# Attention and two feed-forward stages on one core: softmax sums through the row-maximum ring, weights laid out beforehand, Wo prepared during attention

## The chip, the cores and the metric

The kernel runs on one core of one Trainium2 chip. The metric is the device time of one execution in microseconds (us). The core has five engines with queues of their own: TensorE (PE), VectorE (DVE), ScalarE (ACT), GpSimd (POOL) and SyncE (SP, which only issues DMAs here). They meet at semaphores.

## The reference

Input x is 2 x 1024 tokens of 1024 channels, 2048 rows in all, in float32. Three layers follow one another:

```python
x = x + 0.5 * ffn(layernorm(x))      # gate top-2 of 8, base 1024x1024, LoRA rank 16 per expert
x = x + attn(layernorm(x)) @ Wo      # 32 heads of 32, 8 kv heads, RoPE, causal softmax over 1024 keys
x = x + 0.5 * ffn(layernorm(x))      # the same weights again
```

with `ffn(h) = h @ base_w.T + base_b + 2 * sum_e w_e * (h @ A_e.T) @ B_e.T`, where `w` is the softmax over the two largest gate logits, and `attn` computes softmax(q k / sqrt(32)) v for groups of four query heads that share a key and value head.

## The kernel before

Float32 precision is kept by splitting each operand of the large products into a high part (float32r, rounded by ScalarE) and a low part (the rest, by VectorE or GpSimd); `split_products` issues three matmuls for each pair (L48 to L50). Four stages run one after the other: f1 and f2 are `ffn_stage`, between them stand `qkv_stage` and `attention_stage`.

**ffn_stage** goes over 16 tiles of 128 rows. For a tile t: layer norm on VectorE (L520 writes `h`), eight transposes on TensorE (`turn_h`, L360), split into `hT_hi` (ScalarE, L453) and `hT_lo` (VectorE, L524), then the product with the wide weights `wt` (1024 base, 128 LoRA, 8 gate columns = 1160) in three parts of columns, `base(t, ., 2)`, `base(t, ., 0)`, `base(t, ., 1)`, the routing on VectorE, `turn_low`, and `lora`. The weights of part 2 of tile t+1 are used right after `lora(t)`.
- In f1 (`prep`) the weights come as they are given. Ten pieces plus the LoRA up-projection are loaded into `raw`, transposed on TensorE into PSUM (`turn_raw`, L349), and split from there (L448, L499). Only then does `base(0, ., 2)` begin. Both parts are later stored to `copy`, a piece per tile. Tiles also split a piece of `Wq` each.
- In f2 (`attn`) the tile first gets its attention projection, `project`, 48 matmuls with `wo_hi` and `wo_lo`, added to x (L559). Wo is loaded and split at the start of f2, piece by piece (L463, L566), with the projections of tiles 0 and 1 following each piece. The split feed-forward weights are loaded from `copy` during the attention stage.

**attention_stage** takes 16 steps n, one for each pair of batch and key head; a step has 12 units u of up to 512 queries by 128 keys: units 0 to 3 are the first half of the queries, 4 to 11 the second; 0 to 3 and 8 to 11 lie on the diagonal and have 512, 384, 256, 128 queries (4 to 7 have 512). Each unit has four heads g.
- *Row items.* Exponentials need each query's maximum beforehand. For the step n+1, 48 row products (L1232) go into a ring of three PSUM banks (`SLOTS`) and VectorE takes their maxima (L1376); two transposes of the maxima (L1227) go through the same ring. These items are spread over the units of step n.
- *Units.* In the turn of unit u, TensorE issues the scores of unit u+2 (L1242; three banks), each g followed by its portion of row items, and then `products(u)`: four products with the values (L1257) and, for u not in 4 to 7, four with `ones` (L1264) for the softmax sums, each group of four side by side. ScalarE takes exponentials of the scores (L1313) into `probs`, four buffers, unit u in buffer u % 4.
- GpSimd masks the diagonal units (L1165). It adds the buffers of units 4 to 7 (three additions of 128 x 2048, L1187), and their sum is taken by one set of `ones` products at u = 10 (L1269).
- After units 3 and 11 ScalarE copies the context and the sums from PSUM (L1319, L1321). VectorE transposes the sums, takes reciprocals and transposes them back (L1385 to L1391), GpSimd multiplies (`divide`, L1171), ScalarE takes the high part, GpSimd the low part (`low`, L1175), SyncE stores.
The order of each engine's queue is written out by hand; the first step and the last ones stand outside a loop of three steps per pass.

Of the kernel before, what the change touches and what calls it, by code (L numbers as in the profile page):

```python
# [72 lines left out]
def ffn_stage(nc, name, x_src, x_dst, fw, base_b, consts, prep=None, attn=None):  # L73
# [4 lines left out]
    RAW = 4  # L78
    PIECE = KC * D // NT
    COPY = KC * WIDE // NT  # L80
    with ExitStack() as ctx:  # L81
# [5 lines left out]

        (wt_hi, wt_lo), (bt_hi, bt_lo) = fw["wt"], fw["bt"]
        if prep:
            raw = sb("raw", [P, RAW, D], F32)  # L90
            wq_raw = sb("wq_raw", [P, 2, PIECE], F32)
            wq_hi, wq_lo = prep["wq"]
        if attn:
            wo_hi = sb("wo_hi", [P, KC, D], F32R)
            wo_lo = sb("wo_lo", [P, KC, D], F32R)
            ctxT = sb("ctxT", [P, 2, 2, KC, P], F32R)
# [3 lines left out]
        wo_raw = [x_ring[:, 2, :], x_ring[:, 3, :], h[:]]  # L100
# [6 lines left out]
        eps = sb("eps", [P, 1], F32)  # L107
        top = sb("top", [P, 8], F32)
# [35 lines left out]
        turn_ps = [ps[:, 2 * i:2 * i + 2, :].rearrange("p a (c n) -> p (a c) n", n=P) for i in (1, 3)]  # L144


        items = ([("gate", 0), ("A", 0)] + [("base", o) for o in range(KC)] + [("B", 0)]) if prep else []
        EARLY = 2
        TURN_H = 4
        NEXT = 10  # L150

        def raw_count(i):

            return 16 * sum(1 for j in range(i + 1) if j % RAW == i % RAW and items[j][0] != "B")

        x_loaded = [sem(f"x_loaded{s}") for s in range(4)]
        if prep:
            raw_loaded = [sem(f"raw_loaded{s}") for s in range(RAW)]
            b_loaded = sem("b_loaded")
            raw_turned = sem("raw_turned")  # L160
# [4 lines left out]
        if attn:  # L165
            wo_loaded = [sem(f"wo_loaded{s}") for s in range(len(wo_raw))]
# [5 lines left out]
        CONSTS = 2 * 16  # L172
# [34 lines left out]
        def load_ctx(eng, t, par):  # L207
            for part, src in enumerate((attn["ctx_hi"], attn["ctx_lo"])):
                eng.dma_start(ctxT[:, par, part, :, :].bitcast(F32), src[bass.ds(t, 1), :, :, :].rearrange("t c p n -> p (t c) n")).then_inc(ctx_loaded[par], 16)  # L209

        def run_tiles(eng, step):

            with eng.Fori(0, NT // 4 - 1, 1) as i:
# [4 lines left out]

        def turned_view(n, kind):
            v = turn_ps[n % 2]  # L220
            return v[:, :, 0:E] if kind == "gate" else v

        def weight_view(kind, k, part):
            if kind == "base":
# [1244 lines left out]
```

## Time and profile before

| | |
|---|---|
| median of 3 runs | 1725.84 us (1725.3 to 1728.64) |
| the profiled execution | 1721.34 us, its span 1719.4 us |
| granted TensorE clock, mean | 0.965 |
| busy: PE, DVE, ACT, POOL | 1600.4, 937.7, 598.2, 600.4 us |
| stages, from to (us) | f1 0 to about 287, q/k/v to 594, attention to 1281, f2 to 1719 |

In the rows further down a time is measured from the start of the span. A row of the order of time gives the start, the duration, the engine, the line of the kernel, the operation, what it writes and reads with shapes, how many instructions are merged, and in brackets the idle time before it and who ended it.

### The profile page before, as it was taken

Reading aid. Unit: us, or ns where it says so; the run is one execution under the profiler, and the core shown is the slowest. Engines: PE = TensorE matmul, PEld = TensorE weight load, DVE = VectorE, ACT = ScalarE, POOL = GpSimd, SP = SyncE. Lnnn points to the kernel's source line nnn. Section 1 sums busy time; section 2 is a strip of 40 time slices with the busy share of each in tenths; the row PEclk is TensorE's granted clock in tenths of the full one; section 3 lists DMA queues with packets and bytes.
Section 4 is the critical chain, followed back from the end, with each engine's and each line's share of the span. In section 5 each row is a group of like instructions: output and inputs, shape, how many; then the busy total and the mean of one; then the engine's idle time right before and its main releaser. Section 6 shows DMA issues by size and latency. Waiting matters only on the chain. (4 is left out here: it accounts for less than half of the span.)

```text
span 1719.4 us, 30209 instructions
## 1 busy us (share of the span) xinstructions
PE 1600.4 (93%) x9464; PEld 1214.3 (71%) x9464; DVE 937.7 (55%) x2716; ACT 598.2 (35%) x1218; POOL 600.4 (35%) x387
## 2 busy tenths in 40 slices
PE   6999996999999799998998998999949999999999
PEld 5999995788888644444444444454427999999998
DVE  5454444546554477776776777777714333333333
ACT  3333231211120035655555555565543111111110
POOL 1222221433343215665665555555551101101000
PEclk9999997999999869999999999999988999999999
DMA  6333333342331643333333343333135133133130
GB/s 201 131 122 133 133 109 136 118 136 99 110 108 64 163 112 78 90 89 90 90 89 90 92 99 90 89 90 97 47 95 189 54 94 98 49 98 97 49 86 37
DMA packets 167755, 173.69 MB, mean 101 GB/s; under 512 B 50616, under 2 KB 119864, under 8 KB 167616
## 3 DMA queue, kind: packets, MB, share of 16 engines
q1 hardware_dynamic: 139456, 148.90, 30.2%
q10 hardware_dynamic: 28160, 23.07, 4.0%
q8 instruction: 70, 1.15, 0.3%
q14 instruction: 69, 0.57, 0.1%
HBM read 104.24 MB, written 67.17 MB: 100 GB/s over the span
## 5 line engine op out<-in xcount | busy, mean ns | idle before, releaser
L1313 ACT ACTIVATE at_probs<-at_ps 128x512 f32<-128x512 f32 (+3 forms) x768 | 327.0, 495 | 265.9 <-PE at_ps L1242 261.3
L1376 DVE CUSTOM_DVE_ANT_0 at_ps<-at_ps,at_score_mask 128x512 f32<-128x512 f32 (+3 forms) x512 | 292.8, 616 | 98.5 <-PE at_ps L1232 95.5
L1232 PE MATMUL at_ps<-at_ks,at_qs 96*128 96x512 f32 (+3 forms) x768 | 279.6, 389 | 34.2 <-DVE at_part_max L1376 13.1
L1242 PE MATMUL at_ps<-at_qs,at_ks 98*128 98x512 f32 (+3 forms) x768 | 278.5, 389 | 18.6 <-issue 9.6
L1242 PEld LDWEIGHTS at_ps<-at_qs,at_ks 98*128 98x128 f32 x768 | 141.7, 192 | 182.0 <-issue 98.3
L48 PE MATMUL f_ps<-f_wt_hi,f_hT_hi 128*128 128x400 f32 (+1 forms) x768 | 265.5, 346 | 4.8 <-DVE f_wt_lo L499 2.4
L49 PE MATMUL f_ps<-f_wt_lo,f_hT_hi 128*128 128x400 f32 (+1 forms) x768 | 261.4, 340 | 0.0
L50 PE MATMUL f_ps<-f_wt_hi,f_hT_lo 128*128 128x400 f32 (+1 forms) x768 | 261.0, 340 | 0.0
L1232 PEld LDWEIGHTS at_ps<-at_ks,at_qs 96*128 96x128 f32 x768 | 151.8, 198 | 82.5 <-DVE at_part_max L1376 29.4
L317 POOL TENSOR_TENSOR f_x_ring<-f_x_ring,f_half_bias 128x1024 f32<-128x1024 f32 x32 | 76.7, 2396 | 335.6 <-DVE f_h L520 335.1
L1257 PE MATMUL at_ps<-at_probs,at_vs 128*32 128x512 f32 (+3 forms) x1536 | 167.0, 507 | 0.0
L1376 DVE CUSTOM_DVE_ANT_0 at_ps<-at_ps,at_score_mask,at_part_max 128x128 f32<-128x128 f32 (+3 forms) x256 | 133.9, 557 | 59.5 <-PE at_ps L1232 46.1
L1165 POOL TENSOR_SCALAR_AFFINE_SELECT at_probs<-at_probs 128x512 f32<-128x512 f32 x128 | 81.5, 637 | 214.6 <-ACT at_probs L1313 213.7
L48 PEld LDWEIGHTS f_ps<-f_wt_hi,f_hT_hi 128*128 128x128 f32 x768 | 145.4, 189 | 6.6 <-DVE f_wt_lo L499 2.7
L1187 POOL TENSOR_TENSOR at_added<-at_added,at_probs 128x2048 f32<-128x2048 f32 x32 | 146.9, 4591 | 1.5
L49 PEld LDWEIGHTS f_ps<-f_wt_lo,f_hT_hi 128*128 128x128 f32 x768 | 145.7, 190 | 0.6
L50 PEld LDWEIGHTS f_ps<-f_wt_hi,f_hT_lo 128*128 128x128 f32 x768 | 145.1, 189 | 0.0
L48 PE MATMUL f_ps<-f_wo_hi,f_ctxT 128*128 128x512 f32 x256 | 103.3, 403 | 20.0 <-DMA f_ctxT<-scr_ctx_lo 18.8
L48 PE MATMUL qkv_ps<-qkv_hT_hi,wq_hi 128*128 128x512 f32 x256 | 101.5, 396 | 2.4 <-DVE qkv_hT_lo L889 2.4
L49 PE MATMUL f_ps<-f_wo_lo,f_ctxT 128*128 128x512 f32 x256 | 101.2, 395 | 0.0
L50 PE MATMUL f_ps<-f_wo_hi,f_ctxT 128*128 128x512 f32 x256 | 101.2, 395 | 0.0
L50 PE MATMUL qkv_ps<-qkv_hT_hi,wq_lo 128*128 128x512 f32 x256 | 100.3, 392 | 0.0
(123 smaller groups left out, 2402.6 us busy)
## 6 DMA issues: line engine op xcount, KB each, us to landing
at_qs<-scr_q_hi SPq DMA_DIRECT2D x30, 512.0 KB, 6.3
f_x_ring<-in_L_attn_resid SPq DMA_DIRECT2D x16, 512.0 KB, 3.9
x<-f_x_ring SPq DMA_DIRECT2D x16, 512.0 KB, 2.6
qkv_x_ring<-x SPq DMA_DIRECT2D x16, 512.0 KB, 3.3
scr_q_hi<-qkv_rope_hi ACTq DMA_DIRECT2D x32, 256.0 KB, 2.0
scr_q_lo<-qkv_rope_lo ACTq DMA_DIRECT2D x32, 256.0 KB, 2.3
scr_ctx_hi<-at_ctx_hi SPq DMA_DIRECT2D x32, 256.0 KB, 2.2
scr_ctx_lo<-at_ctx_lo SPq DMA_DIRECT2D x32, 256.0 KB, 2.5
```

What stands on the lines that cost most here:

```text
L48: pe.matmul(out, stat_hi, mov_hi, start=start, stop=False)
L49: pe.matmul(out, stat_hi, mov_lo, start=False, stop=False)
L50: return pe.matmul(out, stat_lo, mov_hi, start=False, stop=stop)
L317: pool.tensor_tensor(x_ring[:, u, :], x_ring[:, u, :], half_bias[:], ALU.add).then_inc(bias_added, 1)
L1165: pool.affine_select(out=tile, in_=tile, compare_op=ALU.is_ge, fill=0.0, base=0, pattern=[[0, G], [1, P]], channel_multiplier=-1).then_inc ...
L1187: pool.tensor_tensor(added[:], first, probs[:, u % PROBS, :, :], ALU.add).then_inc(added_done, 1)
L1232: pe.matmul(out[:, 0:keys], qs[0:KROWS, nm, i // QH, g, (i % QH) * P:(i % QH + 1) * P], ks[0:KROWS, nm, c * HALF:c * HALF + keys], start=T ...
L1242: pe.matmul(score_ps[(u * G + g) % BANKS][:, 0:z - a], ks[:, nm, j * P:(j + 1) * P], qs[:, nm, half, g, a - half * HALF:z - half * HALF], ...
L1257: last = pe.matmul(ctx_ps[g * DH:(g + 1) * DH, at], vs[:, nm, j, :], probs[:, u % PROBS, g, 0:z - a], start=j == 0, stop=u in LAST)
L1313: act.activation(probs[:, u % PROBS, g, 0:z - a], score_ps[(u * G + g) % BANKS][:, 0:z - a], ACT.Exp, scale=SCALE).then_inc(exp_done, 1)
L1376: dve.tensor_tensor_reduce(out=src, in0=src, in1=mask, scale=1.0, scalar=part_max[:, g, own] if c else -3.0e38, op0=ALU.add, op1=ALU.max, ...
```

## The change

Two changes are joined.

1. **Feed-forward weights and Wo.** The host lays out base_w, lora_A and gate_w as one matrix of 8 x 128 x 1160 (`ffn_w`), lora_B as 128 x 1024 and Wo by rows. `turn_raw` and everything of it goes. In f1 each of the eight chunks is loaded (`raw_view`, three places and the x ring's last two), split with a factor 0.5 by ScalarE and VectorE, and used at once: `pair_chunk` lets tiles 0 and 1 take each chunk as it comes, in six banks; 16 transposes of the identity go first (`WARM`). The raw layout is copied from DRAM to DRAM in place of the split parts. During attention Wo is loaded, a piece of 256 KB per step, and split by ScalarE (`high_wo`) and GpSimd (`low_wo`); the context of tile 0 is loaded in the last step. f2 starts with the projections of tiles 0 and 1, while the feed-forward weights are loaded and split (`high_landed`, `low_landed`).
2. **Sums.** The sums of a half are one item of the row ring, which has four banks now. `ones` products are no longer part of `products`; GpSimd adds units 0 and 1 (a copy and an addition) and units 4 to 8 (four additions), and one set `sums` before the products of units 3 and 11 takes `added` and the units left apart (2, 3; 9, 10, 11). VectorE transposes the bank itself; the copy L1321 goes. `probs` has five buffers with a table of users.

```diff
-    SLOTS = 3
+    SLOTS = 4
-    PROBS = 4
+    PROBS = 5
-    ADDED = range(4, 8)
-    SUMMED = 10
+        ADDED = {0: 2, 1: 2, 4: 3, 5: 3, 6: 4, 7: 5, 8: 6}
+        APART = ((2, 3), (9, 10, 11))
+        ADDS = 6
+        USERS = ((0, 5, 8), (1, 7), (2, 6, 9), (3, 10), (4, 11))
+        PROB = {u: s for s, users in enumerate(USERS) for u in users}
+        BEFORE = {u: users[i - 1] for users in USERS for i, u in enumerate(users)}
...
+        for u, half in LAST.items():
+            places[u].append(("sum", half))
...
             def exps(n, u, g):
                 if g == 0:
-                    act.wait_ge(unit_done, NU * n + (u + 1))
-                    if u - PROBS in ADDED:
-                        act.wait_ge(added_done, (len(ADDED) - 1) * n + max(u - PROBS - ADDED[0], 1))
+                    v = BEFORE[u]
+                    earlier = NU if v < u else 0
+                    act.wait_ge(unit_done, NU * n + (earlier + 1 + (LAST_OF[units[v][0]] if v in APART[units[v][0]] else v)))
+                    if v in ADDED:
+                        act.wait_ge(added_done, ADDS * n + (ADDED[v] + (ADDS if earlier else 0)))
...
             def add(n, u):
-                pool.wait_ge(exp_done, NU * G * n + (G * (u + 1) + BANKS))
-                if u == ADDED[1]:
-                    pool.wait_ge(unit_done, NU * n + (PROBS + SUMMED + 1 - NU))
-                    first = probs[:, ADDED[0] % PROBS, :, :]
+                here = probs[:, PROB[u], :, :]
+                if u in diagonal:
+                    pool.wait_ge(mask_done, len(diagonal) * n + (diagonal.index(u) + 1))
                 else:
-                    pool.wait_ge(added_done, (len(ADDED) - 1) * n + (u - ADDED[1]))
-                    first = added[:]
-                pool.tensor_tensor(added[:], first, probs[:, u % PROBS, :, :], ALU.add).then_inc(added_done, 1)
+                    pool.wait_ge(exp_done, NU * G * n + (G * (u + 1) + BANKS))
+                if u == 1:
+                    before = probs[:, PROB[0], :, :]
+                    wait_apart(pool, unit_done, NU * n + NU, passed)
+                    pool.tensor_copy(added[:, :, 0:P], before[:, :, 0:P]).then_inc(added_done, 1)
+                    pool.tensor_tensor(added[:, :, P:HALF], before[:, :, P:HALF], here[:, :, 0:HALF - P],
+                                       ALU.add).then_inc(added_done, 1)
+                    return
+                if u == QH + 1:
+                    pool.wait_ge(unit_done, NU * n + (NU + QH))
+                    before = probs[:, PROB[QH], :, :]
+                else:
+                    pool.wait_ge(added_done, ADDS * n + (ADDS + ADDED[u] - 1))
+                    before = added[:]
+                pool.tensor_tensor(added[:], before, here, ALU.add).then_inc(added_done, 1)
...
             def step(n, nm, _, more):   # GpSimd
                 for u in range(NU):
                     a = ahead(n, nm, u, more)
                     if a and a[2] in diagonal:
                         mask(a[0], a[2])
+                    if u == 0:
+                        add(n, 1)
                     if first_step_over(n) and u == 2:
                         divide(n - 1, 1)
-                    if u in (3, 4, 6):
-                        add(n, (5, 6, None, 7)[u - 3])
-                    if first_step_over(n) and u == 8:
+                    if u in (4, 5, 6, 8):
+                        add(n, {4: 5, 5: 6, 6: 7, 8: 8}[u])
+                    if first_step_over(n) and u == 5:
                         low(n - 1, 1)
                     if u == 9:
                         divide(n, 0)
+                    if u == 10:
+                        low_wo(n)
                     if u == 11:
                         low(n, 0)
...
+            def sums(n, half, q, slot):   # TensorE, before products(3) and products(11)
+                pe.wait_ge(slot_read, q + 1)
+                pe.wait_ge(added_done, ADDS * n + (ADDS + (2, ADDS)[half]))
+                pe.wait_ge(mask_done, len(diagonal) * n + (QH * (half + 1)))
+                for g in range(G):
+                    pe.matmul(slot_ps[slot][g * DH:(g + 1) * DH, :], ones[:], added[:, g, :], start=True, stop=False)
+                for u in APART[half]:
+                    a, z = queries(u)
+                    for g in range(G):
+                        last = pe.matmul(slot_ps[slot][g * DH:(g + 1) * DH, a - half * HALF:z - half * HALF], ones[:],
+                                         probs[:, PROB[u], g, 0:z - a], start=False, stop=u == LAST_OF[half])
+                last.then_inc(slot_filled, 1)
...
+            if prep:                      # TensorE, start of f1
+                ALL = (2, 0, 1)
+                for c in range(3):
+                    pair_chunk(0, c, ALL)
+                turn_h(1)
+                for c in range(3, 5):
+                    pair_chunk(0, c, ALL)
+                for c in range(4):
+                    pair_chunk(1, c, (2,))
...
+            if attn:                      # TensorE, start of f2
+                project(0, 0)
+                project(1, 1, first_ps)
```

SyncE, in f1, waits for `w_lo_done` of 1, 2, 3, 5 and 6 low parts before it loads chunks 4, 5, 6, 7 and the LoRA part; in each attention step it waits for `wo_lo_done` of the step before, ahead of the Wo piece.

## Rows read from the trace of the kernel before

**Rows 1.** window of the attention stage: us, busy of PE, PEld, DVE, ACT, POOL

```profile
594.00:1281.00 687.00, 631.85 (x4256) 324.87 (x4256) 486.60 (x1664) 378.64 (x897) 381.54 (x240) 0.96 0.36 89
```

**Rows 2.** TensorE in order of time, stage f1: start us, us, engine, line, out<-in

```profile
55.87 1.03 PE L360 MATMUL f_ps<-f_ident,f_h 128*128 128x128 f32 x8
...
71.02 1.04 PE L360 MATMUL f_ps<-f_ident,f_h 128*128 128x128 f32 x8
```

**Rows 3.** SyncE's queue, VectorE and TensorE in order of time, start of stage f2

```profile
1281.58 0.34 SPq L242 DMA_DIRECT2D f_ident<-in_identity  x1
...
1307.79 1.29 DVE L559 TENSOR_TENSOR f_x_ring<-f_ps,f_x_ring 128x512 f32<-128x512 f32 x2 [2.59 <-DMA f_x_ring<-x]
...
1311.31 0.81 DVE L520 TENSOR_SCALAR f_h<-f_x_ring,f_mv,f_rstd 128x1024 f32<-128x1024 f32 x1
...
1317.66 1.03 PE L360 MATMUL f_ps<-f_ident,f_h 128*128 128x128 f32 x8
...
1321.07 0.43 PE L48 MATMUL f_ps<-f_wt_hi,f_hT_hi 128*128 128x360 f32 x1 [2.37 <-DVE f_hT_lo L524]
...
1325.14 1.03 PE L360 MATMUL f_ps<-f_ident,f_h 128*128 128x128 f32 x8
...
1351.18 1.04 PE L360 MATMUL f_ps<-f_ident,f_h 128*128 128x128 f32 x8
```

**Rows 4.** DMA issues of the page: KB each, median us to landing

```profile
f_x_ring<-in_L_attn_resid SPq DMA_DIRECT2D x16, 512.0 KB, 3.9
```

**Rows 5.** groups of instructions by shape: busy us, mean ns of one, idle us before them

```profile
L1232 PE MATMUL at_ps<-at_ks,at_qs 96*128 96x256 f32 x128 | 41.3, 350 | 12.2 <-DVE at_part_max L1376 9.2 <-DVE at_neg_lo L1362 2.8
...
L566 DVE TENSOR_TENSOR f_wo_lo<-f_x_ring,f_wo_hi 128x1024 fp32r<-128x1024 f32 x6 | 7.4, 1226 | 19.2 <-ACT f_wo_hi L463 19.1
```

**Rows 6.** windows, the loads at the start of f1: last columns PEclk, DMA share, GB/s

```profile
5.00:10.00 5.00, 3.42 (x18) 2.96 (x19) 0.23 (x1) 2.03 (x3) 0.00 (x0) 1.00 0.93 333
```

**Rows 7.** TensorE in order of time, a steady attention step and the last one

```profile
868.34 0.41 PE L1242 MATMUL at_ps<-at_qs,at_ks 98*128 98x512 f32 x1
...
886.08 0.50 PE L1242 MATMUL at_ps<-at_qs,at_ks 98*128 98x512 f32 x1
...
1269.70 1.04 PE L1269 MATMUL at_ps<-at_added,at_ones 128*32 128x512 f32 x8
...
1270.56 0.40 PE L1257 MATMUL at_ps<-at_probs,at_vs 128*32 128x128 f32 x8
```

**Rows 8.** GpSimd in order of time, steady attention steps and the last one

```profile
846.57 4.68 POOL L1187 TENSOR_TENSOR at_added<-at_probs 128x2048 f32<-128x2048 f32 x1 [2.89 <-ACT at_probs L1313]
...
856.50 4.59 POOL L1187 TENSOR_TENSOR at_added<-at_added,at_probs 128x2048 f32<-128x2048 f32 x1
...
861.04 0.63 POOL L1165 TENSOR_SCALAR_AFFINE_SELECT at_probs<-at_probs 128x512 f32<-128x512 f32 x1
...
862.45 1.28 POOL L1175 TENSOR_TENSOR at_ctx_lo<-at_ctxn,at_ctx_hi 128x512 fp32r<-128x512 f32 x1
...
886.43 4.68 POOL L1187 TENSOR_TENSOR at_added<-at_probs 128x2048 f32<-128x2048 f32 x1 [2.73 <-ACT at_probs L1313]
...
930.12 4.69 POOL L1187 TENSOR_TENSOR at_added<-at_probs 128x2048 f32<-128x2048 f32 x1 [2.90 <-ACT at_probs L1313]
...
1252.34 4.68 POOL L1187 TENSOR_TENSOR at_added<-at_probs 128x2048 f32<-128x2048 f32 x1 [5.27 <-ACT at_probs L1313]
```

**Rows 9.** ScalarE in order of time, first exponentials of a step

```profile
867.59 2.07 ACT L1313 ACTIVATE at_probs<-at_ps 128x512 f32<-128x512 f32 x4 [2.29 <-PE at_ps L1242]
```

**Rows 10.** TensorE in order of time, two rows after longer idles

```profile
39.13 1.43 PE L360 MATMUL f_ps<-f_ident,f_h 128*128 128x128 f32 x8 [2.87 <-DVE f_bt_lo L503]
...
915.85 0.38 PE L1242 MATMUL at_ps<-at_qs,at_ks 98*128 98x256 f32 x1 [3.00 <-issue]
```

**Rows 11.** windows, granted clock in the column PEclk

```profile
917.00:918.00 1.00, 1.00 (x4) 0.91 (x4) 0.79 (x5) 0.57 (x3) 0.00 (x0) 0.50 0.72 197
...
1320.00:1325.00 5.00, 3.93 (x24) 3.93 (x25) 3.39 (x6) 1.58 (x2) 0.98 (x1) 1.00 0.00 0
```

More of the change, by code:

```diff
@@ L278, in _ @@
             if prep:
-                sp.wait_ge(w_lo_done, len(items))
-                for part in range(2):
-                    sp.dma_start(prep["copy"]["bt"][part], flat(fw["bt"][part]).bitcast(F32)).then_inc(copy_stored, 16)
+                sp.dma_start(prep["copy"]["bt"], prep["ffn_bt"]).then_inc(copy_stored, 16)
             def step(i, t, u, more):
@@ L377, in base, with pair_chunk @@
                     last.then_inc(gl_done, 1)
+            def pair_chunk(t, c, parts):
+                pe.wait_ge(hT_lo_done, t + 1)
+                pe.wait_ge(w_lo_done, c + 1)
+                for part in parts:
+                    cols = slice(PARTS[part].start, WIDE if part == 2 else PARTS[part].stop)
+                    last = split_products(pe, pair_ps[t][part], hT_hi[:, t, c, :], hT_lo[:, t, c, :],
+                                          wt_hi[:, c, cols], wt_lo[:, c, cols], c == 0, part == 2 and c == KC - 1)
+                    if part == 2 and c == KC - 1:
+                        last.then_inc(gl_done, 1)
             def turn_low(t, more):
@@ L1053, in portions @@
         def portions(u, items):
+            items = [(p, it) for p, it in items if it[0] != "sum"]
             n = len(items)
@@ L1131, in _ @@
             load_rows(0, 0, at_a)
-            for part in range(2):
-                sp.dma_start(flat(fw["bt"][part]).bitcast(F32), copy["bt"][part]).then_inc(fw_loaded, 16)
             def step(n, nm, _, more):
@@ L1137, in step @@
                 if more >= 2:
-                    sp.wait_ge(unit_done, NU * n + PROBS)
+                    sp.wait_ge(unit_done, NU * n + NU)
                     load(n + 2, (nm + 2) % RING)
-                for part in range(2):
-                    sp.dma_start(flat(fw["wt"][part])[:, bass.ds(n * PIECE, PIECE)].bitcast(F32),
-                                 copy["wt"][part][:, bass.ds(n * PIECE, PIECE)]).then_inc(fw_loaded, 16)
+                sp.wait_ge(wo_lo_done, n + 1)
+                sp.dma_start(wo_raw[:], wo_src[:, bass.ds(n * PIECE, PIECE)]).then_inc(wo_loaded, 16)
+                if not more:
+                    for half in range(2):
+                        sp.wait_ge(ctx_stored[half], 32 * NKV + 16)
+                    for part, name in enumerate(("ctx_hi", "ctx_lo")):
+                        sp.dma_start(first_ctx[:, part, :, :].bitcast(F32), scr[name][0].rearrange("c p n -> p c n")).then_inc(ctx_loaded, 16)
                 if more:
@@ L1209, in _ @@
             low(NG - 1, 1)
+            pool.wait_ge(wo_lo_done, NG + 1)
         @block.tensor
         def _(pe):
[L1213 removed]
+            for count, start in ((slot_read, SLOTS), (exp_done, BANKS), (unit_done, NU), (added_done, ADDS), (recipT_done, 1),
                                  (ctx_copied, 1), (recip_done, 1), (mult_done, 1), (rows_loaded[0], 16),
@@ L1295, in step @@
                         slot_items(g)
+                    if u in LAST:
+                        p = position(("sum", LAST[u]), more)
+                        sums(n, LAST[u], SEQ * n + (PRE + p), (PRE + SEQ * nm + p) % SLOTS)
                     products(n, nm, u)
```

508 lines of the change are left out of this document (280 added, 228 removed).

## The prediction, made before the changed kernel was run

> **What bounds the kernel now.** I read four views: the busy shares by stage, the waits, the order of time at both feed-forward starts, and one steady attention step on each engine. In the attention stage TensorE is busy for 632 of 687 us, VectorE for 487, GpSimd for 382 [rows 1]: TensorE sets the pace, with GpSimd at 56%. At the start of f1 it is another limit: TensorE transposes weights and waits for their splitting. The bulk of the two feed-forward stages and the q/k/v stage is TensorE back to back and isn't changed. So the change has three places: the start of stage f1, the attention step (16 times), and the start of stage f2.
>
> **Start of f1.** Removed: ten weight pieces through TensorE transposes and PSUM, loaded before tile 1's work could begin. The marker is the set of eight transposes of tile 3, now at 71.02; a steady tile takes 71.02 - 55.87 = 15.15 us [rows 2]. Before that marker TensorE must, after the change, do tiles 0 and 1 (30.3) and the first product part of tile 2 (about 3.9, the stretch from 1321.07 to the transposes ending the part, 1325.14 [rows 3]): 34.2 us. The earliest start: x issued at about 1.3 and landing 3.9 later [rows 4], a layer norm of 3.0 (the 4.3 from 1307.79 to the end of the row at 1311.31, less two additions of 0.65), then 3.4 from transposes to first product (1317.66 to 1321.07) [rows 3]: 11.6. If TensorE never waited, the marker would stand at 45.8. It will wait: VectorE makes nine low parts of about 1.39 us (1.226 for 1024 columns [rows 5], times 1160/1024), beside two layer norms and two splits of transposed tiles, and the raw ring has four places, so chunks 4 to 7 are loaded only as low parts finish. By that list chunk 3 is ready at 18.4, chunk 4 at 19.8, chunk 7 at 27, and TensorE is continuous from about 22. That adds 2.7. The loads are no limit: 333 GB/s was reached between 5 and 10 us [rows 6], 1.8 us for a chunk of 594 KB. Marker at 48.5, gain 22.5 us. Bounds: 45.8 gives 25; if every chunk waits 1 us more for its load, 17.
>
> **Start of f2.** Before, the stage begins with Wo loads at 1281.58 and reaches tile 1's transposes at 1325.14, 43.6 later [rows 3]; most of this is Wo landing and being split. Wo now is ready. TensorE starts at about +2.2 (the identity), and two projections follow. One costs 26.04 - 15.15 = 10.9 us (the f2 tile period, 1325.14 to 1351.18, less that of f1 [rows 2, 3]); the first gets 2 more for a low clock at the start (the granted clock is 0.50 to 1.00 after an idle, below). They end at +15.1 and, with tile 0's transposes, +27.0. Then VectorE is late: from +15.1 addition and norm (3.7), three low parts (4.2), the split of the transposed tile (1.2), three low parts (4.2), addition (1.3), the small low part (1.2), norm (3.0): +33.9, so tile 1's transposes at +34.1. Gain 9.4. Bounds: 6 if the loads of 6.8 MB run at 200 instead of 333 GB/s, 11 if VectorE's order costs less.
>
> **Attention: what goes.** A step loses two product sets with `ones`, one of 512 columns (0.86 us, 1269.70 to 1270.56 [rows 7]) and one of 384 (three quarters, 0.65): 1.5 us. The fourth bank removes part of the short waits for row maxima: the row items of 256 columns alone waited 12.2 us in 16 steps [rows 5], 0.76 a step, and I take 1.0 for all. If TensorE stayed the limit, a step would fall from 39.86 (846.57 to 886.43 [rows 8]) to about 37.3. ScalarE loses 2 copies of the sums and gains one Wo piece; it has pauses before its exponentials (2.29 [rows 9]) that cover this. SyncE's Wo load of 256 KB replaces 580 KB of weights; its new wait on `wo_lo_done` is for work of the step before. Behind it stand only row loads and stores, which come later.
>
> **Attention: what comes.** GpSimd gets a copy of 512 columns and an addition of 1536 for units 0 and 1, a fourth addition of 2048 for unit 8, and the low part of Wo. By rows that is 0.64 to 1.28 (a mask or a two-input row of 512 [rows 8]), 3.4, 4.55 and 1.28: about 10 more on 24, 34 of 39.9 us. That fits, so the total isn't the limit; I take 0.8 for the copy, which hides in either case. The Trainium skill, GPSIMD Engine Reference, section Engine selection, says that two-input elementwise work is about twice as slow on GpSimd as on VectorE and one-input work about line rate. The trace agrees as far as it goes: 0.63 for a mask of 512 columns, 1.28 for a two-input row of 512. By it the copy would be at the lower end, the sum stays as it is, and moving additions here is what it speaks against.
>
> What matters is the order. `exps` of unit 0 of the next step writes buffer 0, last used by unit 8 (`USERS`), so it now waits for the addition of unit 8, the last of the step. The first addition of the half, of units 4 and 5, waits for `unit_done` of unit 3, whose products now stand behind the first sum set. So a chain runs on GpSimd: additions 5 and 6 and mask 8 (846.57 to 856.50: 9.93), `low` of the step before (1.28, moved ahead from u = 8), addition 7 (856.50 to 861.04: 4.54), masks 9 and 10 (0.61 each), addition 8 (4.54): 21.5 us [rows 8]. TensorE's own way over that stretch, from the scores of unit 6 (886.08 [rows 7]) to ScalarE's first exponential of unit 0 (867.59 plus a step, 907.45 [rows 9]), is 21.4 before and about 19 after the sets of units 8 and 9 and the waits have gone. GpSimd arrives 2.6 us later. TensorE holds three score banks, so the fourth score of unit 0 stands until the first exponential is done. Queued behind it are all row items, and so VectorE.
>
> The rest of the loop is TensorE's: that fourth score (868.34) to the scores of unit 6 (886.08), 17.74 [rows 7]. Sets worth 3.67 us leave this part and sets worth 3.67 (1280 columns for half 1, 896 for half 0) enter it; four banks take away most of its waits, which I put at 0.8 of the 1.0 (the 256-column items lie here). The loop is 0.1 + 21.5 + 0.1 (to ScalarE) + 0.75 (exponential, to score four) + 17.74 - 0.8 + 0.1 = 39.5. So against 39.86 almost all the 1.5 us saved on TensorE is spent on waiting for GpSimd.
>
> **The clock.** An idle of 2.37 us before 1321.07 [rows 3] left the granted clock at 1.00 in that stretch [rows 11], 2.4 GHz; one of 3.00 before 915.85 [rows 10] was followed by 0.50, 1.2 GHz [rows 11], and after one of 2.87 before 39.13 [rows 10] eight transposes took 1.43 in place of 1.03 [rows 2], the like sign. The step around the second took 930.12 - 886.43 = 43.69 [rows 8], 3.83 over a plain one, so the fall cost 0.8 over its idle. The new idle, 2.0 to 3.1, lies between. I take a fall in about half of the steps at 1.0: a step of 40.0, +0.15. Fifteen intervals: +2.
>
> **The end of attention.** In the last step no rows stand between the sets. There 18.9 us lie between addition 5 and the last products (1252.34 [rows 8] to about 1271.2 [rows 7]); after, 21.5 + 0.6 (mask 11) + 2.15 + 0.25 = 24.5. VectorE transposing straight from the bank gives back about 2, and step 0 loses 0.65: +3.
>
> **Sum.** -22.5 - 9.4 + 2 + 3 = -27. The profiled execution took 1721.34 (span 1719.4) and would take 1694.5. The median of the runs, 1725.84, is 4.5 above it: 1699.
>
> **Rivals.** (1) TensorE stays the limit, the GpSimd chain being hidden: 15 x -2.55 = -38, less 32 at the starts, 3 back: 1659. For it: GpSimd is only 56% busy now. Against: addition times are steady at 4.54 to 4.69 [rows 8], and the chain counts them one by one. (2) GpSimd's chain with the clock never falling: 15 x -0.35 = -5 in place of +2: 1692. Falling every time at the full 1.0: 1707. (3) The starts give half, because loads and splits queue behind each other: 16 less gained, 1715. For it: ring places 4 to 7 depend on low parts. Against: 333 GB/s [rows 6]. (4) Slower: the low clock after each GpSimd stall outlasts the step's free part and hits products at half rate for 5 us, 2.5 lost each time; with the step at 42.0, 15 x 2.15 = +32 and 3, less 32: 1729. It decides above 2.1 us per step. Against: the marked fall cost 0.8.
>
> **Chances.** The GpSimd chain as forecast, clock between never and always falling (1692 to 1707): 70%. TensorE the limit, or nearly (1659 to 1685): 10%. Starts worth half: 14%. Slower: 3%. No gain measurable: 3%. The range 1680 to 1715 leaves out the far end of the first rival and the last two. Changes under 0.2% (3.5 us) aren't told from none: faster 94%, same 3%, slower 3%.
>
> **What would show it.** After: ScalarE idle before `at_probs` released by GpSimd `at_added`, about 2.5 us once a step; additions 5 to 8 nearly unbroken; a step period of 39.5 to 40.5; tile 3's transposes in f1 near 48.5; tile 1's in f2 some 34 after the stage's first load; granted clock under 1.00 behind some stalls. Wrong if the period is near 37 (the chain is shorter or starts earlier than unit 3's products), or if f1's marker is past 54.

## The result, and the profile after the change

The changed kernel takes 1749.35 us (median, 1743.87 to 1754.05), the kernel before 1727.24 on the same chips (1725.30 to 1728.88): ratio 1.0127, 95% interval 1.0094 to 1.0161 (further down, ratios have their interval in brackets). It is 1.3% slower, where 1.6% faster was predicted. The profiled execution has a span of 1748.9 us, 29.5 more than before.

The page of the changed kernel: span, busy us of each engine, TensorE's busy share and granted clock in 40 slices.

```profile
span 1748.9 us, 29557 instructions
...
PE 1602.6 (92%) x9136; PEld 1219.4 (70%) x9136; DVE 950.9 (54%) x2707; ACT 591.9 (34%) x1199; POOL 755.4 (43%) x451
...
PE   7999995999999799989889898999967999999999
...
PEclk9999996999999579898897888888888999999999
```

TensorE looks as busy as before, but the last row shows why this says little: through attention (slices 15 to 31) the granted clock is 0.7 to 0.9, and at half rate the same matmuls are busy for nearly twice as long (the eight of one sum set 1.94 us from 1138.32, 1.06 from 1109.02).

Where the time went, by markers: the first addition of units 4 and 5 starts at 625.31, 16.5 us earlier than before (641.86); from that addition to the same one of the last step it takes 655.85 us in place of 610.48, +45.4 (15 steps, a mean of 43.72 for 40.70); from there to f2's first load 34.8 in place of 29.2, +5.5; f2's start -6.6 (below); the rest of f2 +1.7. Together +29.5. So both starts gained, and attention lost twice as much as they brought.

One plain step of attention. GpSimd, ScalarE and TensorE in order of time (start us, us, engine, line, operation; in brackets the idle before and what ended it):

```profile
1111.07 4.69 POOL L1286 TENSOR_TENSOR at_added<-at_probs 128x2048 f32<-128x2048 f32 x1 [2.84 <-PE at_ps L1366]
1115.84 4.62 POOL L1286 TENSOR_TENSOR at_added<-at_added,at_probs 128x2048 f32<-128x2048 f32 x1
1120.42 1.28 POOL L1263 TENSOR_TENSOR at_ctx_lo<-at_ctxn,at_ctx_hi 128x512 fp32r<-128x512 f32 x1
1121.66 0.62 POOL L1253 TENSOR_SCALAR_AFFINE_SELECT at_probs<-at_probs 128x512 f32<-128x512 f32 x1
1122.27 4.59 POOL L1286 TENSOR_TENSOR at_added<-at_added,at_probs 128x2048 f32<-128x2048 f32 x1
1126.82 1.21 POOL L1253 TENSOR_SCALAR_AFFINE_SELECT at_probs<-at_probs 128x512 f32<-128x512 f32 x2
1128.01 4.52 POOL L1286 TENSOR_TENSOR at_added<-at_added,at_probs 128x2048 f32<-128x2048 f32 x1
...
1132.64 1.58 ACT L1430 ACTIVATE at_probs<-at_ps 128x512 f32<-128x512 f32 x3 [5.65 <-POOL at_added L1286]
...
1133.29 0.80 PE L1351 MATMUL at_ps<-at_qs,at_ks 98*128 98x512 f32 x1 [3.59 <-ACT at_probs L1430]
...
1154.18 4.69 POOL L1286 TENSOR_TENSOR at_added<-at_probs 128x2048 f32<-128x2048 f32 x1 [2.69 <-PE at_ps L1366]
```

This is the predicted chain: additions 5 to 8, a low part and masks without a pause from 1111.07 to 1132.5, then the exponential of the next step's unit 0, then the fourth score. Its length to ScalarE is 21.57 us (predicted 21.5 + 0.1). The other part of the loop, from ScalarE to the next step's addition of units 4 and 5, is 21.54 us where 17.9 was predicted. The windows show what it is made of (columns: stretch, its length, busy us of PE, PEld, DVE, ACT, POOL, granted clock, DMA share, GB/s):

```profile
1108.00:1112.00 4.00, 4.00 (x42) 2.30 (x41) 2.96 (x8) 2.67 (x6) 1.16 (x2) 1.00 1.08 236
1128.00:1132.00 4.00, 1.71 (x13) 0.86 (x5) 2.09 (x7) 0.00 (x0) 4.00 (x2) 1.00 0.00 0
1132.00:1136.00 4.00, 2.71 (x12) 1.25 (x13) 0.82 (x2) 2.60 (x5) 3.47 (x5) 0.52 0.00 0
1136.00:1140.00 4.00, 4.00 (x15) 1.98 (x17) 2.31 (x6) 1.85 (x4) 2.12 (x3) 0.50 0.01 4
1140.00:1144.00 4.00, 4.00 (x44) 2.20 (x37) 1.15 (x5) 1.04 (x4) 0.52 (x1) 0.70 0.44 131
1144.00:1148.00 4.00, 4.00 (x29) 1.99 (x30) 3.31 (x18) 1.73 (x8) 3.08 (x3) 1.00 0.15 39
```

After the idle of 3.59 us TensorE stands at 0.50 (1.2 GHz) and comes back to 1.00 only at about 1142, though it is busy without a break from 1133.29 on: some 9 us in which the products of unit 10, the next step's scores, row items and the sum set of half 1 go at half rate. This step is one of the worse ones. Of the 15, the clock stands at 0.50 for 10.2 us in five and for 6.8 in ten (688.4 to 695.2, for one). The waits of attention:

```profile
PE at_ps L1351 <- ACT at_probs L1430: 54.4, 20, 3.6
...
ACT at_probs L1430 <- POOL at_added L1286: 95.4, 28, 5.7
```

TensorE idles once in each of the 15 steps ahead of the same score, 2.94 us in the first and 3.54 to 3.59 in the others: 53 of the 54.4 us.

The two starts of the feed-forward stages, TensorE and SyncE in order of time:

```profile
36.97 0.33 PE L371 MATMUL f_ps<-f_ident,f_low_s 128*128 128x128 f32 x1 [2.34 <-DVE f_low_s L590]
...
52.95 1.06 PE L336 MATMUL f_ps<-f_ident,f_h 128*128 128x128 f32 x8 [1.08 <-DVE f_x_ring L630]
...
1315.93 0.35 SPq L238 DMA_DIRECT2D f_ident<-in_identity  x1
...
1317.83 0.79 PE L48 MATMUL f_ps<-wo_hi,first_ctx 128*128 128x512 f32 x1 [10.52 <-DMA f_ident<-in_identity]
...
1352.93 1.96 PE L336 MATMUL f_ps<-f_ident,f_h 128*128 128x128 f32 x8 [4.79 <-DVE f_h L560]
```

Tile 3's transposes of f1 stand at 52.95, 18.1 us earlier than before [rows 2] (22.5 predicted). Tile 1's of f2 come 37.0 us after the stage's first load, 43.56 before [rows 3], a gain of 6.6 (9.4 predicted): VectorE is the late one, as predicted, but its norm is 2.9 us later.

### The profile page after: what moved, and what is told of

Its sections match the earlier page's. It is cut to its first block and busy times, and to the rows that moved or that the text cites. A ratio compares the mean times of both kernels' runs of the same rounds, so it can differ in the third digit from the quotient of the medians.

```text
span 1748.9 us, 29557 instructions
## 1 busy us (share of the span) xinstructions
PE 1602.6 (92%) x9136; PEld 1219.4 (70%) x9136; DVE 950.9 (54%) x2707; ACT 591.9 (34%) x1199; POOL 755.4 (43%) x451
## 5 line engine op out<-in xcount | busy, mean ns | idle before, releaser
L1430 ACT ACTIVATE at_probs<-at_ps 128x512 f32<-128x512 f32 (+3 forms) x768 | 330.8, 494 | 241.8 <-PE at_ps L1351 140.8
L1351 PE MATMUL at_ps<-at_qs,at_ks 98*128 98x512 f32 (+3 forms) x768 | 297.4, 414 | 68.1 <-ACT at_probs L1430 58.5
L1351 PEld LDWEIGHTS at_ps<-at_qs,at_ks 98*128 98x128 f32 x768 | 154.0, 209 | 234.8 <-ACT at_probs L1430 181.0
L1286 POOL TENSOR_TENSOR at_added<-at_added,at_probs 128x2048 f32<-128x2048 f32 x48 | 220.2, 4588 | 1.5
L1341 PEld LDWEIGHTS at_ps<-at_ks,at_qs 96*128 96x128 f32 x768 | 162.1, 215 | 39.2 <-issue 12.4
L1366 PE MATMUL at_ps<-at_probs,at_vs 128*32 128x512 f32 (+3 forms) x1536 | 175.1, 531 | 9.0 <-POOL at_probs L1253 9.0
L1286 POOL TENSOR_TENSOR at_added<-at_probs 128x2048 f32<-128x2048 f32 x16 | 75.2, 4700 | 61.7 <-PE at_ps L1366 61.7
L49 PE MATMUL qkv_ps<-qkv_hT_lo,wq_hi 128*128 128x512 f32 x256 | 100.2, 392 | 0.0
L931 POOL TENSOR_TENSOR qkv_rot<-qkv_rot,qkv_sin 128x512 f32<-128x512 f32 x40 | 51.5, 1289 | 106.2 <-DVE qkv_rot L987 106.1
```

The lines of the kernel that those rows point to most:

```text
L49: pe.matmul(out, stat_hi, mov_lo, start=False, stop=False)
L931: pool.tensor_tensor(rot[:, g % 2, :], rot[:, g % 2, :], sin[:, cols], ALU.mult).then_inc(sin_done, 1)
L1286: pool.tensor_tensor(added[:], before, here, ALU.add).then_inc(added_done, 1)
L1341: pe.matmul(out[:, 0:keys], qs[0:KROWS, nm, i // QH, g, (i % QH) * P:(i % QH + 1) * P], ks[0:KROWS, nm, c * HALF:c * HALF + keys], start=T ...
L1351: pe.matmul(score_ps[(u * G + g) % BANKS][:, 0:z - a], ks[:, nm, j * P:(j + 1) * P], qs[:, nm, half, g, a - half * HALF:z - half * HALF], ...
L1366: last = pe.matmul(ctx_ps[g * DH:(g + 1) * DH, at], vs[:, nm, j, :], probs[:, PROB[u], g, 0:z - a], start=j == 0, stop=u in LAST)
```

## The experiments

Five theories ran against each other. **A**: the loss is GpSimd's chain, waited for once a step, and the clock that falls behind each wait. **B**: the additions are in the way wherever the wait stands. **C**: the four banks and the sum items slow the ring. **D**: the clock's fall costs nothing of its own. **E**: splitting Wo in attention costs the steps. Each ratio is to the kernel before, run beside it. A step is the time from one step's addition of units 4 and 5 to the next one's; "plain" leaves out the three ends of the loop's turns. The runs are from several chips, and the kernel before took 1725.4 to 1727.2 us beside all of them.

**Fill the idle time (D).** Ahead of the fourth score of unit 0, the one that waits:

```
if a and a[2] == 0 and g == G - 1:
    ...
    pe.wait_ge(slot_read, SEQ * n + (PRE + p) + 1)
    for _ in range(FILL):    # 14, or 7
        pe.matmul(slot_ps[...], ks[0:KROWS, nm, 0:P], qs[0:KROWS, nm, 1, 0, :], start=True, stop=True)
```

> The changed kernel with 14 spare products of 512 columns (about 3 us) into the row bank that is free at that point, ahead of the fourth score of unit 0 of the next step, the one that stands and waits. They change no result and lengthen TensorE's own work, but fill most of the idle time. Theory A: the GpSimd chain and the wait stay (step 39.5 to 40.2), but the clock stays at 1.00: 15 x 2.2 to 3 less, 1704 to 1716. Rival D (the clock's fall costs nothing of its own, since the step's length is that of the additions all the way round): within 5 us of 1749. If the spare products only add to TensorE's work: 1750 to 1795.

1701.09 us, ratio 0.9847 (0.9826 to 0.9869): 48 us below the changed kernel, by work that nobody needs. TensorE in order of time, and the windows over the same stretch:

```profile
1132.24 3.38 PE L1410 MATMUL at_ps<-at_qs,at_ks 96*128 96x512 f32 x14
1136.05 0.50 PE L1352 MATMUL at_ps<-at_qs,at_ks 98*128 98x512 f32 x1 [0.43 <-ACT at_probs L1437]
```

```profile
1132.00:1136.00 4.00, 3.62 (x16) 2.63 (x14) 1.41 (x4) 0.60 (x2) 4.00 (x3) 1.00 0.00 0
1136.00:1140.00 4.00, 3.95 (x29) 1.99 (x33) 2.49 (x7) 3.51 (x8) 3.33 (x4) 1.00 0.00 0
```

The score still waits for GpSimd, but the clock stays at 1.00, and the plain step is 39.3 us (additions at 1113.72 and 1153.05; 39.2 to 39.4 but for the first and the last), against 42.1 to 43.3 in the changed kernel; the prediction had put the loop at 39.5 with the clock kept. From the fourth score to the next step's first addition it is 17.0 us here (1136.05 to 1153.05) and 20.9 in the changed kernel (1133.29 to 1154.18), for the same products: the fall costs 3.9 us there and 3.2 in the mean step (43.72 for 40.51). Plain step by plain step it is 3.6 to 4.0 where the clock is low for 10.2 us and 2.8 to 3.2 where it is for 6.8. D is out.

> The changed kernel with 7 spare products (1.5 us) in place of 14 ahead of the score that waits, so that an idle of about 2.1 us is left in each step. Theory A: it is the idle's length that decides; 2.37 us left the clock alone at the start of f2, 2.94 with the low part moved did not: here it stays, 1698 to 1710. If it falls in some of the steps: 1710 to 1735. If any idle lowers it: 1735 to 1750.

1733.59 us, ratio 1.0044 (1.0026 to 1.0063; the ratio leaves out one of the ten runs, which took 5055.75 us, has no trace and stays unexplained; the median of the other nine is 1731.93). The idle left was 1.37 us in the first step and 1.96 to 2.03 in the others. The two steps of these windows had idles of 2.03 and 2.02 (ahead of 1115.11 and 1154.22):

```profile
1117.00:1121.00 4.00, 4.00 (x48) 2.05 (x47) 2.53 (x7) 1.83 (x6) 3.46 (x4) 1.00 0.01 4
1154.00:1158.00 4.00, 3.78 (x16) 2.40 (x17) 1.29 (x3) 3.32 (x8) 3.18 (x4) 0.60 0.00 0
```

The clock fell behind 11 of the 14 idles of about 2 us, for 3.4 or 6.8 us, and stayed behind three, the one ahead of 1115.11 among them. The expectation that 2 us are harmless was wrong; the middle one, a fall in some of the steps, gives the time.

**The wait itself.** First a sixth buffer, paid for with the 8 KB of f2's first context tile (f2 then loads that itself, and its first product comes 6.6 us after the stage's first load, not 1.9):

```
-    PROBS = 5
+    PROBS = 6
-    USERS = ((0, 5, 8), (1, 7), (2, 6, 9), (3, 10), (4, 11))
+    USERS = ((0, 6), (1, 7), (2, 8), (3, 9), (4, 10), (5, 11))
```

> The changed kernel with a sixth probability buffer (unit u in buffer u modulo 6), so that unit 0 of the next step follows unit 6 and no longer waits for the addition of unit 8; the 8 KB come from the context tile that attention loaded ahead for stage f2, which f2 now loads itself. Theory A (the changed kernel is slow because unit 0 of the next step waits for the additions 5 to 8 on GpSimd, and the gap of 3.6 us lowers the clock each time): gap and fall both vanish, TensorE is the limit again, the step goes from 42.6 to 37.3 to 38.5 us, 15 x 4.1 to 5.3 = 62 to 80 us less, 2 back at the start of f2: 1670 to 1690. Rival B (the additions on GpSimd are in the way wherever the wait stands, since the sum set of half 1 needs the addition of unit 8 too): the gap moves to that set, step 41 to 43, 1730 to 1752. Rival C (the five slower us of a step come from four row-maximum banks and the sum items in the ring, not from the buffers): within 5 us of 1749.

Then only another table for the five: `USERS = ((0, 7), (1, 5, 8), (2, 6, 9), (3, 10), (4, 11))`.

> The changed kernel with one line of its buffer table changed: users (0, 7) and (1, 5, 8) in place of (0, 5, 8) and (1, 7). Unit 0 of the next step now waits for the addition of unit 7, and unit 1 of the next step for that of unit 8. Theory A: unit 0 comes 4.5 us earlier, so without a stall; unit 1 follows it on TensorE by about 3.5 us, so at most about 1 us of stall is left, in two smaller parts, too short for a fall of the clock: step 38.5 to 40, 1749 - 15 x (2.6 to 4.1) = 1688 to 1710. Rivals B and C: within 5 us of 1749.

1730.93 us, 1.0026 (1.0006 to 1.0047), and 1728.21 us, 1.0011 (0.9993 to 1.0028): 18 and 21 us below the changed kernel, where A said 59 to 79 and 39 to 61. B looked the better theory. But with six buffers the wait for `at_added` was gone from ScalarE's list, yet TensorE idled 3.5 us a step as before (the waits of ScalarE and of TensorE):

```profile
ACT at_ctx_hi L1435 <- POOL at_ctxn L1253: 52.6, 15, 3.6
...
PE at_ps L1345 <- ACT at_probs L1424: 54.0, 20, 3.6
```

`high(n, 0)` stands in ScalarE's order ahead of the exponentials of the next unit 1, waits for GpSimd's `divide`, and `divide` stands behind the addition of unit 8. It is a second way from the same chain, hidden by the first. Hence two kernels that cut both: the one with six buffers, with `divide(n, 0)` ahead of the addition of unit 8, and the one with the other table, with `high(n, 0)` at u = 11:

> The six-buffer kernel with GpSimd's multiplication of half 0 by the reciprocals moved ahead of the addition of unit 8. In the six-buffer run unit 0 no longer waited, but ScalarE's high part of half 0 (queued ahead of the exponentials of unit 1 of the next step) waited 3.6 us a step for this multiplication, which stood behind the addition of unit 8. Theory A2 (two waits lead from GpSimd's additions into ScalarE's order; taking away one alone leaves the other, with the same gap and the same fall of the clock): now neither is left, TensorE is the limit: step 37.3 to 38.3, 1731 - 15 x 3.3 to 4.5, 1663 to 1682. Rival B2 (a third wait on the additions comes up, at the sum set of half 1): step 39 to 41.5, 1690 to 1730. Rival C (ring of four banks and sum items are slow by themselves): 1725 to 1735.

> The kernel with the changed buffer table (five buffers) and ScalarE's high part of half 0 moved behind the exponentials of unit 1 of the next step, so that nothing of the next step stands behind the multiplication. Left is the wait of unit 1 of the next step for the addition of unit 8, which was 1.0 us long for ScalarE. Theory A2: step 38 to 39.3, no fall of the clock, 1728 - 15 x 2 to 3.5 = 1675 to 1698. Rivals B2 and C: 1720 to 1735.

1697.42 us, 0.9845 (0.9823 to 0.9868), and 1709.66 us, 0.9914 (0.9886 to 0.9942). Rival B2 was right for the first: TensorE now waited 1.97 us a step at the sum set of half 1, for the mask of unit 11 behind the addition of unit 8. The second lies between A2 and its rivals, with waits of 1.3 us for unit 8's addition and of 2.0 to 2.6 us for a row load in some steps.

**The low part.** One line back to where it was before the change, behind the addition of unit 8 (`low(n - 1, 1)` at u = 8 in place of 5):

> The changed kernel with the low part of the step before (1.28 us on GpSimd) put back behind the addition of unit 8, where it was before the change: the chain of GpSimd is 1.28 us shorter, nothing else is altered. Theory A: 15 x 1.28 = 19 us less, 1730, and if the gap of then 2.3 us no longer lowers the clock, as one of 2.37 did not, 15 x 2.4 more, 1694. Rivals B and C: within 5 us of 1749.

> The same, with the low part of the step before also behind the addition of unit 8, so that this addition ends 1.28 us earlier and the 1.0 us wait of unit 1 goes. Theory A2: 0 to 15 us below the kernel without this move; the two at the same time if TensorE sets the step in both: 1668 to 1695.

1731.44 us, 1.0027 (1.0014 to 1.0041), 18 us less where 15 x 1.28 gives 19, with the clock falling behind idles of 2.77 to 2.95 just the same; as A said for that case. On the table with the moved high part: 1697.49 us, 0.9864 (0.9824 to 0.9905), 12 us less and just above the forecast.

**The third way.** Six buffers, high part at u = 11, low part behind the mask of unit 11:

> The six-buffer kernel with every other work moved out from ahead of what waits for GpSimd: ScalarE's high part of half 0 behind the exponentials of unit 1 of the next step, GpSimd's low part of the step before behind the mask of unit 11, its multiplication where the changed kernel has it. In the run with the earlier multiplication TensorE still waited 1.97 us a step ahead of the sum set of half 1, for GpSimd's mask of unit 11, behind the low part, the multiplication and the addition of unit 8; here that mask comes 2.6 us earlier. Theory A3 (all that the changed kernel loses in attention is waiting for GpSimd's chain and the clock that it costs): plain steps of 37.3 to 37.8, the ends of the loop's turns 41 to 44 as in all kernels, mean 38.4: 1697 - 20 = 1670 to 1690. Rival (the step is bound elsewhere too): 1690 to 1700.

1700.54 us, 0.9839 (0.9818 to 0.9860): the rival, not A3. One new wait was left. TensorE, SyncE and GpSimd in order of time:

```profile
1096.78 0.28 PE L1330 MATMUL at_ps<-at_ident,at_row_max 128*16 128x128 f32 x1
...
1098.30 1.27 POOL L1257 TENSOR_TENSOR at_ctx_lo<-at_ctxn,at_ctx_hi 128x512 fp32r<-128x512 f32 x1
...
1099.99 0.37 SPq L1208 DMA_DIRECT2D scr_ctx_hi<-at_ctx_hi  x1
1100.46 0.45 SPq L1208 DMA_DIRECT2D scr_ctx_lo<-at_ctx_lo  x1
1101.04 0.52 SPq L1201 DMA_DIRECT2D at_qs<-at_neg_hi  x1
1101.60 0.59 SPq L1201 DMA_DIRECT2D at_qs<-at_neg_lo  x1
...
1103.55 0.73 PE L1345 MATMUL at_ps<-at_qs,at_ks 98*128 98x512 f32 x2 [1.92 <-DMA at_qs<-at_neg_lo]
```

The maxima of half 1 are turned at 1096.78, but SyncE issues their row load at 1101.04, because the store of half 0 stands ahead of it and waits for GpSimd's low part. The edit puts the store behind that load:

```
     def step(n, nm, _, more):
         load_rows(nm, 1, ...)
+        if first_step_over(n):
+            store(n - 1, 0)
...
-        store(n, 0)
```

> The six-buffer kernel with all waits moved, and SyncE's store of half 0 moved from the end of the step to behind the next step's load of the rows of half 1. In the kernel without this move TensorE waits 1.9 to 2.5 us a step for that row load, whose rows were turned 4 us earlier but whose issue stands behind the store of half 0, and the store waits for GpSimd's low part of half 0, the last of its chain. Theory A4 (a third way leads from GpSimd's additions to TensorE, through SyncE's order): the gap goes, plain steps of 37.3 to 37.8 throughout, mean 38.3, 1700 - 15 x 1.3 to 1.6 = 1675 to 1684. Rival G (the row load is late by its own way, from the turn over ScalarE and VectorE): the gap stays over 1 us, 1694 to 1702.

> The same three moves (high part of half 0 behind the exponentials of unit 1 of the next step, low part of the step before behind the mask of unit 11, store of half 0 behind the next row load) with the five buffers of the changed kernel in the other table, and f2's first context tile loaded ahead as in the changed kernel. Against the six-buffer kernel f2's start is 4.7 us shorter (first product 1.9 us after the stage's first load, in place of 6.6), and unit 1 of the next step waits up to 1 us for the addition of unit 8. Theory A4: 1672 to 1690. Rival G: 1690 to 1700.

1650.41 us, 0.9563 (0.9550 to 0.9576), and with five buffers 1658.62 us, 0.9610 (0.9596 to 0.9624): 4.4% and 3.9% faster than the kernel before. A4 is confirmed and G is out; both times lie below A4's range, by 25 and 13 us, because A4 still took the prediction's 37.3 us for TensorE's own step. B in its plain form is out too: all the additions are still there. With six buffers, TensorE's waits in attention, and the window of one plain step:

```profile
PE at_ps L1347 <- issue: 8.9, 3, 3.1
PE at_ps L1347 <- ACT at_probs L1426: 7.9, 15, 1.0
PE at_ps L1372 <- POOL at_probs L1249: 4.5, 14, 0.3
PE at_ps L1347 <- DMA at_qs<-at_neg_lo: 2.0, 4, 0.7
```

```profile
1106.74:1142.35 35.61, 34.81 (x251) 19.07 (x251) 30.02 (x105) 22.94 (x56) 33.50 (x20) 1.00 0.28 71
```

No wait above 1 us in a plain step, the clock at 1.00 in all of it, 35.4 us for most steps, with GpSimd busy for 33.5. Taken one by one the cuts tell the order in which the ways hide each other:

> The changed kernel with the moved store of half 0 alone. In the changed kernel the row load isn't waited for (1.2 us in all in attention), since the wait of unit 0 for the addition of unit 8 comes later and covers it. Theory A4 (several ways lead from the chain, and the longest hides the others): no effect, 1740 to 1752. Rival H (the 50 us came from the store's place as such): 1690 to 1705.

> The five-buffer kernel of the last pair with all three moves, but with the changed kernel's own buffer table, so that unit 0 of the next step waits for the addition of unit 8 again. Theory A4: this one wait alone brings back the chain (21.5 - 1.3 of the low part, then TensorE's 17.7), a gap of 2.9 us and the fall behind it, as in the kernel with the low part moved: 1722 to 1735, some 70 us above the kernel with the other table. Rival H: 1658 to 1670.

The moved store alone: 1746.76 us, 1.0124 (1.0102 to 1.0145). All three moves without the table: 1723.99 us, 0.9988 (0.9975 to 1.0001), 65 us above the same kernel with it. So the store is worth nothing while the buffer waits, and 50 us (1700.54 to 1650.41) when it is the last.

**The fourth bank (C).** Three banks in place of four, first in the kernel that still had the row wait, then in the fastest:

> The same kernel with three row-maximum banks in place of four, the sum items still in the ring. If the fourth bank is worth what the prediction took, 1.0 us of a step: 15 us slower than with four, 1692. Since the two sum items now hold one bank of three, up to 2 us a step: up to 1710. If the banks aren't what TensorE waits for: within 3 us of the kernel with four.

> The six-buffer kernel with the moved store, with three row-maximum banks in place of four. Now nothing else covers TensorE's waits for row maxima. The prediction put the fourth bank at 1.0 us of a step: 15 us, 1665. In the earlier pair plain steps without any gap were 38.6 us with three banks; if those are TensorE's steps with three banks, against 35.4 with four: 15 x 3.2 = 48 us, 1698.

1704.97 us, 0.9867 (0.9844 to 0.9890), and 1699.55 us, 0.9832 (0.9802 to 0.9862). C is out: four banks are 49 us faster than three where nothing covers them, 3.0 us of a plain step (38.4 for 35.4). In the covered kernel only 4 us of it could be seen.

**The old attention (E).**

> The changed kernel with the attention of before: three row-maximum banks, a bank for the sums, four buffers, additions of units 4 to 7 alone; what stays of the change is stage f1's start, the pieces of Wo split during attention, and stage f2's start. By the traces f1 and the q/k/v stage came 16.8 us earlier and f2's start was 6.6 us shorter: 1727 - 23 = 1699 to 1709. If the split of Wo in attention cost the changed kernel its steps (rival E): 1715 to 1750.

1703.97 us, 0.9882 (0.9858 to 0.9905), and its plain steps are 39.8 to 40.1 us, as before the change. E is out; the two starts bring 21.5 us (1725.44 of its kernel before, less 1703.97).

**The start of f1.** `routing(0, 0)` ahead of `layer_norm(0, 2, 2)` on VectorE, and `gap_exp(0)` ahead of `deviation(2)` on ScalarE, in the kernel of six buffers and the old store:

> The kernel with all waits moved, and at the start of stage f1 the routing of tile 0 ahead of the layer norm of tile 2 on VectorE (and its exponential ahead of the square root on ScalarE). TensorE waited 2.34 us at 36.97 for this routing. Theory F (this order costs 2.3 of the 4.4 us by which tile 3's transposes came later than predicted): tile 3's transposes at 50.5 to 51.5 in place of 52.95, time 1 to 2.5 us less. Rival (the norm of tile 2 is then late for its transposes): at 52 to 55, no gain.

1699.16 us, 0.9843 (0.9823 to 0.9863), no difference. The wait at 36.97 shrank to 0.36 us, and this came in its place, with the clock at half rate behind it (0.54 for matmuls of 0.34):

```profile
39.72 0.67 PE L48 MATMUL f_ps<-f_bt_hi,f_lowT_hi 128*128 128x400 f32 x1 [2.75 <-DVE f_lowT_lo L619]
40.19 0.54 PE L49 MATMUL f_ps<-f_bt_lo,f_lowT_hi 128*128 128x400 f32 x1
...
56.70 1.06 PE L336 MATMUL f_ps<-f_ident,f_h 128*128 128x128 f32 x8 [1.08 <-DVE f_x_ring L630]
```

Tile 3's transposes went from 54.33 to 56.70, past what either theory gave. Theory F is wrong: the routing of tile 0 and the low part after it are one chain, and with the norm between them the other link is waited for. Both ahead of the norm was not tried.

## Why the prediction was wrong

**The failed step is the clock.** The prediction took "a fall in about half of the steps at 1.0", +0.15 a step over the kernel before. The clock fell in every step and cost 3.2 us of the mean one: 15 x (3.2 - 0.5) = 41 us. Its price came from one fall [rows 8, 10], behind which the clock was low for 3.4 us. The attention stage of before has three such falls, all at ends of the loop's turns, and the one that was not read was the dearest: an idle of 3.43 us, 6.8 us at half rate, and a step of 44.91 us, so 1.6 over its idle by the prediction's own way of counting (44.91 - 39.86 - 3.43). TensorE, GpSimd and a window, before:

```profile
791.70 0.58 PE L1242 MATMUL at_ps<-at_qs,at_ks 98*128 98x256 f32 x1 [3.43 <-issue]
...
761.84 4.68 POOL L1187 TENSOR_TENSOR at_added<-at_probs 128x2048 f32<-128x2048 f32 x1 [2.74 <-ACT at_probs L1313]
806.75 4.68 POOL L1187 TENSOR_TENSOR at_added<-at_probs 128x2048 f32<-128x2048 f32 x1 [2.89 <-ACT at_probs L1313]
...
791.00:797.00 6.00, 5.30 (x26) 2.85 (x26) 2.17 (x11) 1.69 (x5) 0.64 (x1) 0.50 0.42 120
```

In the changed kernel the clock is low for 6.8 to 10.2 us, over just the part of the loop that is TensorE's own: GpSimd's next chain starts after the products of unit 3, so each microsecond lost between the wait and those products lengthens the step. The price to take was about half of that stretch, 3.4 us and up, and not what a fall had cost elsewhere; 2.8 to 4.0 were measured. The idle, "2.0 to 3.1", was 3.6, for a reason given below.

In the traces the changed kernel ends 56 us behind the forecast (1748.9 for 1719.4 - 27). The clock makes 41 of them, the starts by their markers 9 (16.5 and 6.6 in place of 31.9), the end of attention 2.5, and the rest is spread out. The medians are only 50 apart, as the profiled execution of before was 6 us below its median.

The Trainium skill, TensorE: Matmul & The Clock Gate, section HAM oscillation, describes this pattern for a loop that waits for a DMA: where the wait of every turn is long enough, each turn starts cold and pays the transition again. The trace agrees, in 15 of 15 steps, with GpSimd as the one waited for.

**Right.** The chain and its place: 21.57 us for 21.5. The loop with the clock kept: 39.3 for 39.5, which the spare products showed. The rival on the other side was the right mechanism, at 1729 and a chance of 3%: it asked for 2.1 us a step to be slower, and the step got 3.0.

**The end of attention.** +5.5 in place of +3: TensorE waits 4.45 us ahead of the last sum set (at 1303.30), and the clock is at 0.50 from 1299.4 to 1306.2.

**The starts.** 21.5 us in place of 31.9 by the kernel with the old attention (23.1 by the markers). In f1, 4.4 are missing at the marker: three waits for VectorE of 2.34, 1.08 and 0.87 us make 4.3, where TensorE was taken to be continuous. (The first product part of tile 2, put at 3.9, is 4.07 by its own rows.) In f2, 2.9 are missing, since VectorE's three low parts before the second addition took 6.96 us with their waits, not 4.2. The starts thus gave two thirds of the forecast, where the rival at 14% had a half; alone that makes 1709.

**TensorE's own step.** Put at 37.3 (39.86 - 1.5 - 1.0), it is 35.4, or 39.86 - 1.5 - 3.0: the sum products were sized rightly (38.4 is left with three banks, 39.86 - 1.5), the fourth bank was sized by the listed waits at 1.0 us and is worth 3.0. The waits in the list aren't all of it: with three banks the records show TensorE 1.8 us busier a step too (36.59 for 34.81), for the same products; why is left open. So the price of waiting for GpSimd was higher than the prediction knew, 39.3 - 35.4 = 3.9 us before the clock.

**What wasn't seen.** The prediction named one way from the chain to TensorE. The runs found four: the buffer of unit 8, `high` behind `divide`, the mask of unit 11, and the store of half 0 ahead of the row load. In the changed kernel only the first shows, so this did not make the number wrong, but with the first alone cut the kernel is still no faster than before (ratios 1.0026 and 1.0011).

## What to carry to other kernels

Price a stall in a loop together with the clock behind it, and as a full loss if the late engine's next start depends on TensorE's work there; a spare matmul in the gap is a cheap test of how much is the clock. When work moves to a slower engine, follow everything queued behind it on every queue, the DMA queue's stores too: late ways hide one another, and cutting one proves little until the rest are cut. A resource whose waits are covered (the fourth bank) shows its worth only when the cover is gone.

## What the runs showed of the hardware

An idle of about 2 us can go either way. In f1 the changed kernel and the kernel with six buffers run the same instructions; windows from 37 to 40 us, first of the changed kernel, then of the one with six buffers and the old store, behind idles of 2.34 and 2.17 us:

```profile
37.00:40.00 3.00, 3.00 (x17) 2.88 (x18) 2.02 (x9) 2.62 (x4) 0.00 (x0) 1.00 0.00 0
```

```profile
37.00:40.00 3.00, 3.00 (x10) 2.97 (x11) 2.01 (x9) 2.48 (x4) 0.00 (x0) 0.50 0.00 0
```

The longer idle left the clock at 1.00, the shorter one halved it, and tile 3's transposes came 1.4 us later for it (54.33 for 52.95). In the kernel with six buffers and the earlier multiplication, behind idles of 1.97 us at the sum set, the clock fell in some steps (0.65 from 972 to 976) and stayed in others (1.00 from 1052 to 1056). Even behind idles of 1.28 to 1.32 us (other table, high part moved) it fell in five of twelve cases, 0.50 from 975.8 to 979.1 for one. Behind the 30 idles of 2.77 to 3.59 us at the fourth score, in the changed kernel and the one with the low part moved, it fell every time and stood at 0.50 for 3.4 to 10.2 us. Why it goes one way or the other at 1.3 to 2.3 us is left open.

GpSimd's prices came out near those that the nearest rows gave: a copy of 512 columns 0.61 us (0.8 taken), an addition of 1536 columns 3.55 (3.4), of 2048 columns 4.51 to 4.72 (4.55).
